# Row maxima of four attention heads: transposed at full array width and placed with one DMA

## The reference

```python
qkv = layernorm(x) @ w_attn + b_attn                # q, k, v: 32 heads of 16
scores = einsum('bqhd,bkhd->bhqk', q, k) / 16
scores = where(causal, scores + slope[h] * (k_pos - q_pos), -inf)
x = x + softmax(scores) @ v @ w_proj + b_proj
x = x + (silu(h @ w_gate.T) * (h @ w_up.T)) @ w_down.T     # h = layernorm(x)
```

## Time and profile before

| what | value |
|---|---|
| median of 3 executions | 840.43 us (840.23 to 841.11) |
| span of the profiled execution | 840.8 us |
| its own time | not given apart from the span, which lies among the three |
| TensorE busy | 789.2 us, 94% |
| VectorE, ScalarE, GpSimd busy | 646.3, 415.4, 296.3 us |
| mean granted TensorE clock | 0.994 of full |

### The profile page before, as it was taken

How to read it: one execution, slowest core, us unless ns; L and a number is a source line. 1 busy time by engine, 2 the same in 40 slices (tenths; PEclk the granted TensorE clock), 3 DMA queues, 4 the chain that set the end, 5 groups by cost and what they waited for, 6 DMA issues and landing times.

```text
span 840.8 us, 13423 instructions
## 1 busy us (share of the span) xinstructions
PE 789.2 (94%) x4554; PEld 543.8 (65%) x4554; DVE 646.3 (77%) x1609; ACT 415.4 (49%) x796; POOL 296.3 (35%) x435
## 2 busy tenths in 40 slices
PE   3899899999999999999998899999998999999998
PEld 2655455556555565555554477888876778888886
DVE  6497788878888888878887156849998787888764
ACT  4335666665666656565666524324336334334441
POOL 6223234342443424423433403324450034443342
PEclk9999999999999999999999999999999999999999
DMA  8873656556575575737563416041214422221052
GB/s 281 228 228 110 180 165 204 183 159 200 166 241 151 157 220 168 240 111 229 188 194 104 155 69 217 3 172 40 75 50 148 166 78 85 76 76 51 13 161 102
DMA packets 76332, 122.80 MB, mean 146 GB/s; under 512 B 14035, under 2 KB 39302, under 8 KB 76265
## 3 DMA queue, kind: packets, MB, share of 16 engines
q1 hardware_dynamic: 74217, 121.69, 45.9%
q10 hardware_dynamic: 2048, 0.27, 0.2%
HBM read 79.34 MB, written 42.32 MB: 145 GB/s over the span
## 4 chain that ended last, share of the span: by engine, by line
PE 62%; DVE 20%; DMA 6%; ACT 4%; issue 4%; POOL 2%; SPq 1%; ACTq 0%; DVEq 0%
PE bank L1282 19%; PE bank L1918 10%; PE bank L1201 7%; PE bank L1127 6%; PE bank L1184 6%; PE bank L1159 5%; PE bank L1112 5%; DVE bank L920 3%; PE bank L1116 3%; ACT pt L749 2%; DMA pv_dram<-weighed 2%; DVE stats L176 1%; POOL scratch L648 1%; DVE scratch L892 1%; PE bank L1094 1%
## 5 line engine op out<-in xcount | busy, mean ns | idle before, releaser
L749 ACT ACTIVATE pt<-bank 128x512 f32<-128x512 f32 (+1 forms) x384 | 193.8, 529 | 132.4 <-PE bank L1184 121.4
L920 DVE CUSTOM_DVE_ANT_0 bank<-bank,mask_qk 128x512 f32<-128x512 f32 (+3 forms) x416 | 195.9, 511 | 47.5 <-PE bank L1159 45.7
L1184 PE MATMUL bank<-q_st,k_st 116*128 116x512 bf16 (+3 forms) x512 | 133.6, 304 | 15.5 <-ACT pt L749 13.5
L1159 PE MATMUL bank<-k_st,q_st 97*128 97x512 bf16 (+3 forms) x512 | 133.1, 307 | 6.6 <-DMA q_st<-slopes_dram 4.3
L1513 POOL TENSOR_TENSOR wd_lo<-wd_raw,wd_hi 128x512 fp32r<-128x512 f32 x33 | 44.4, 1350 | 161.8 <-ACT wd_hi L1543 161.8
L654 POOL TENSOR_SCALAR_AFFINE_SELECT pt<-pt 128x256 f32<-128x256 f32 x128 | 55.6, 434 | 129.7 <-ACT pt L749 129.7
L1159 PEld LDWEIGHTS bank<-k_st,q_st 97*128 97x128 bf16 x512 | 42.2, 99 | 68.7 <-issue 38.4
L658 POOL TENSOR_SCALAR_AFFINE_SELECT pt<-pt 128x256 f32<-128x256 f32 x128 | 53.3, 416 | 77.0 <-ACT pt L749 76.7
L1201 PE MATMUL bank<-pt,v_nat 128*32 128x512 f32 (+3 forms) x1024 | 76.9, 441 | 3.0 <-POOL pt L654 2.3
L1184 PEld LDWEIGHTS bank<-q_st,k_st 116*128 116x128 bf16 x512 | 44.7, 98 | 47.3 <-ACT pt L749 23.5
L1918 PE MATMUL bank<-wd_hi,w_hi 128*128 128x512 f32 x176 | 70.0, 398 | 4.8 <-DVE wd_lo L1695 2.0
(11 more groups left out here) (185 smaller groups left out, 1714.8 us busy)
## 6 DMA issues: line engine op xcount, KB each, us to landing
stack_dram<-scratch SPq DMA_DIRECT2D x32, 384.0 KB, 3.1
q_st<-stack_dram SPq DMA_DIRECT2D x32, 384.0 KB
k_st<-stack_dram SPq DMA_DIRECT2D x32, 384.0 KB
wd_raw<-w_down SPq DMA_DIRECT2D x44, 256.0 KB, 3.5
xt<-w_gate_up SPq DMA_DIRECT2D x20, 512.0 KB, 3.7
stack_dram<-scratch SPq DMA_DIRECT2D x32, 256.0 KB, 3.6
pv_dram<-weighed SPq DMA_DIRECT2D x32, 256.0 KB, 4.4
weighed<-pv_dram SPq DMA_DIRECT2D x17, 256.0 KB
```

The lines of the kernel that those rows point to most:

```text
L749: act.activation(pt[:, h % PT_RING, COL0[k]:COL0[k] + WIDE[k]], bank[3 + (3 * h + k) % 2][:, 0:WIDE[k]], ACT.Exp, scale=1.0 / HD).then_inc ...
L920: last = dve.tensor_tensor_reduce(bank[k][:, at:at + n], bank[k][:, at:at + n], mask_qk[:, S - n:S], 1.0, NEG, ALU.add, ALU.max, mx[:, h % ...
L1159: last = pe.matmul(bank[k][:, at:at + n], q_st[0:K_MAX, s, h % 4, t * P:(t + 1) * P], k_st[0:K_MAX, s, h % 4, 0:n], start=True, stop=not b ...
L1184: last = pe.matmul(bank[3 + u % 2][:, at:at + n], k_st[0:K_EXP, s, h % 4, t * P:(t + 1) * P], q_st[0:K_EXP, s, h % 4, t * P:S], start=True ...
```

## The change

The 32 columns of `mparts` become the first columns of a 128-column tile `maxima`, whose other 96 columns are cleared once at the start by one more GpSimd memset. The transpose takes all 128 columns and writes 128 partitions of bank 6, the last 96 of them zeros. The copy takes the first 32 partitions, as before, to an `mt` with one buffer, and waits for the landing of the chunk before. One DMA takes 32 partitions of `mt` to rows 97 and 99, with one semaphore in place of two.

```diff
         mx = sb("mx", [P, 4, TT])
-        mparts = sb("mparts", [P, 2, 4 * TT], BF16)
-        mt = sb("mt", [2 * 4 * TT, 2, P], BF16)
+        maxima = sb("maxima", [P, P], BF16)
+        mparts = maxima[:, 0:2 * 4 * TT].rearrange("p (a n) -> p a n", a=2)
+        mt = sb("mt", [2 * 4 * TT, P], BF16)
...
-        m_placed = [sem(f"m_placed{i}") for i in range(2)]
+        m_placed = sem("m_placed")
...
-            pool.wait_ge(zeroed, 5)
+            pool.memset(maxima[:, :], 0.0).then_inc(zeroed, 1)
+            pool.wait_ge(zeroed, 6)
...
             def place_maxima(c):
-                n = 4 * TT
                 act.wait_ge(m_copied, c + 1)
-                for a in range(2):
-                    row = ROW_X + 1 + 2 * a
-                    act.dma_start(q_st[row:row + 1, c % SLOTS, :, :].rearrange("p h (t n) -> p (h t) n", n=P),
-                                  mt[a * n:(a + 1) * n, c % 2, :]).then_inc(m_placed[c % 2], 16)
+                act.dma_start(q_st[ROW_X + 1:K_SUM:2, c % SLOTS, :, :].rearrange("p h (t n) -> p (h t) n", n=P),
+                              mt[:, :]).then_inc(m_placed, 16)
...
             def copy_maxima(c):
                 dve.wait_ge(m_done, c + 1)
-                need(dve, m_placed[c % 2], c // 2 * 32)
-                dve.tensor_copy(mt[:, c % 2, :], bank[6][0:2 * 4 * TT, 0:P // 2].bitcast(BF16)).then_inc(m_copied, 1)
+                need(dve, m_placed, c * 16)
+                dve.tensor_copy(mt[:, :], bank[6][0:2 * 4 * TT, 0:P // 2].bitcast(BF16)).then_inc(m_copied, 1)
...
-                pe.transpose(bank[6][0:2 * 4 * TT, 0:P // 2].bitcast(BF16),
-                             mparts[:, :, :].rearrange("p a n -> p (a n)"), identb[:, :]).then_inc(m_done, 1)
+                pe.transpose(bank[6][:, 0:P // 2].bitcast(BF16), maxima[:, :], identb[:, :]).then_inc(m_done, 1)
...
                 if h % 4 == 0 and k == 0:
-                    pe.wait_ge(m_placed[c % 2], (c // 2 + 1) * 32)
+                    pe.wait_ge(m_placed, (c + 1) * 16)
```

## The result

The changed kernel took 837.8 us against 844.4 us of the kernel before, measured side by side in 20 executions each. The two medians differ by 6.5 us; the ratio of the executions is 0.993, with a 95% interval of 0.991 to 0.995, which is 5.9 us less. On other chips it gave 0.9924 (0.9894 to 0.9954) and 0.9938 (0.9910 to 0.9966). The forecast was 833 us, 0.9% less; the range, 829.5 to 838.5, holds the median by 0.7 us, though the kernel before itself came out 4 us higher than the 840.4 it was counted from. So the time itself tells little: rival 1's 837.0 lies nearer to it than the forecast. What tells the two apart is the difference and the profiles.

What follows compares the result with a forecast made beforehand. TensorE, busy 94% of the span and carrying 62% of the chain, was taken as the bound. Savings of 3.9 + 0.2 + 2.4 + 1.0 = 7.5 us from 840.4 gave 833 us, range 829.5 to 838.5.

Steps and rivals of the forecast that it cites:

- rival 1: The gap around TensorE's transpose comes from the bank or wait instructions, not the strip; 837.0 us, chance 0.12.
- Term 1: On TensorE, a full-width transpose avoids the 32-column strip's price: 0.195 us each at 20 chain places, 3.9 us, plus 0.2.
- Term 2: On ScalarE, one DMA issue in place of two saves 0.6 us at four places on the chain, 2.4 us.
- Term 3: Near 98 us, TensorE's wait for the placing's landing shrinks with one DMA: 1.0 us, between 0.55 and 1.35.
- Rival 2: The single placing DMA, shared by fewer DMA engines, lands late and costs time; about 844 us, chance 0.07.
- Rival 3: Half-clock stretches in the last chunks: one or both vanish, 831.3 or 829.6 (chance 0.12), or a third comes, 834.7 (0.06).

## Why the prediction was right

**Term 1, the transpose: right in its mechanism and in the size of one.** 0.26 us a transpose before and 0.06 after. At six of the 32 places, chunks 11, 12, 19, 20, 27 and 28, the distance shrank only to 0.29 to 0.32 us; what holds it there is open. The steady stretch gave 3.5 us, as the 18 transposes that the chain has in it times 0.195. The match is closer than the evidence: the three changed profiles have 310.8 to 312.7 us there without late round trips, and the full-width transpose with two DMAs 313.3. The division of the array was named as the cause from the strip products; 32, 64 and 128 columns, and one and two transposes, bear it out. The rule of the Trainium skill (TensorEngine Tiling (Array Packing), Key Properties) agrees, and these runs give its price here: about 0.10 us on the way in and 0.10 on the way out. Rival 1 is out: bank and waits were the same with the wide transpose, and the gap was gone.

**Term 2, the issue: the mechanism right, the size too high.** Forecast 0.6 us at each of four places, 2.4 in all. The kernel with the full-width transpose and two DMAs, beside the changed one, takes it alone. It is 0.5 us at each of the two places from 28 to 31 (34.9 against 33.9 us), because the single issue takes 0.62 us where the pair's took 0.51 and 0.60. It is 0.34 near 86 us (11.43 against 11.09 from transpose 3 to 4). Near 461 us it is 0.37 (6.70 against 6.33 from transpose 31 to the next value product). That makes 1.7 us.

**Term 3, the landing: the size right, its cause in part open.** 1.35 and 1.7 us of waiting before, 0.18, 0.19 and 0.35 in the three changed profiles: 1.0 to 1.5 for the 1.0 that was taken. But the wait is not the second DMA's alone. It is 0.40 us with two DMAs and the full-width transpose, 1.8 with two and the strip issued twice, 0.45 and 0.47 with one DMA and a strip, and 1.34 with one DMA and the full-width transpose issued twice. The last piece of this placing came 3.9 to 5.5 us after the first issue in the four profiles with two DMAs, 3.7 to 4.3 in six with one and 5.05 in a seventh. Over all chunks the medians are 3.2 to 3.5 us with two and 2.7 to 2.9 with one: the half microsecond that the forecast named is there, and this one placing scatters by more. The stretch from 1 to 5, with term 3 and one place of term 2 in it, gave 2.4 us for 2.0.

**Rival 2, the late landing, did not come,** but what it was built on did. The DMA queue of ScalarE moved 1088 pieces, as its page above has it, in place of the 2048 on the page of the kernel before:

```profile
q10 hardware_dynamic: 2048, 0.27, 0.2%
```

Sixteen pieces behind one another take some 0.3 us in most chunks, up to 1.3 in some. In the three changed profiles the last of them was moved 1.5 to 5.1 us after the issue, 2.8 in the median, where the rival needed a landing at 5.4 everywhere. One chunk of the kernel with its transpose issued twice has 5.7.

**Rival 3, the clock: partly seen, and no gain of the whole.** The kernel before has a half-clock stretch between transposes 28 and 31 in both profiles, the changed one in none of three. From 28 to 31 the kernel gained 2.4 us. The two parts by themselves, in kernels that have no half clock there either, make 1.2 us of it, as forecast: the strip costs 0.2 (34.1 against 33.9) and the second issue 1.0. The other 1.2 of the 2.4 is the clock's. But two of the three have it just behind transpose 31, and the part from there to the end is 1.1 us longer. In these two it was moved, not removed.

**The sum.** 3.5 for the steady stretch, 2.4 from 1 to 5, 2.4 from 28 to 31, less 1.1 behind it, is 7.2 us, against 7.5 forecast. That it comes so near is in part luck: the last two parts gave 1.2 more and 1.9 less than forecast, by where half-clock stretches fell. The three ratios give 5.2 to 6.4 us, and their intervals reach from 2.9 to 8.9. If the difference from 7.2 is more than scatter, the late round trips may be the place: mostly about 1.3 us each, and the changed profiles have one or two.

**What the forecast missed** is the scatter. It took 840.4 from three executions as the kernel's time; over 20 it was 844.4. Its upper bound, too, is 838.7 by its own terms (840.4 less 1.7), not 838.5. The start alone, up to the first transpose, varies from 46.4 to 50.9 us between profiles, a chunk with a late round trip by up to 3, the part behind transpose 31 by some 1.5 for each half-clock stretch.

## What to carry to other kernels

A small matmul that divides the array differently from its neighbours pays for the switch twice, on the way in and on the way out; this was measured here for a bf16 transpose of 128 rows and 32 or 64 columns. Look at the distance of starts around it, not at its own duration, and fill it up to its neighbours' width where the extra columns are free. Where a small transfer hangs behind a wait, count how often the engine that issues it, or its landing, is on the chain before taking a gain for it: here 4 and 1 of 32. Being on the chain is not the whole price: of four issues taken at 0.6 us, two gave 0.5 and two less than 0.4. And cut a profile into stretches at an instruction that recurs; parts of a change that the whole's scatter hides can be read there to a tenth of a microsecond where the stretch is short and holds no wait for a DMA and no half clock (11.16 and 10.66 us from transpose 29 to 30), and no better than 1 to 2 us over the long one from 5 to 28.

## What the runs showed of the hardware that was not expected

- A 64-column division costs as much as a 32-column one (0.44 us of spacing against 0.23 undivided), and a second transpose of the same division costs its columns only, 0.05 to 0.06 us.
- An 8 KB placing issued some 3 us later in a chunk was done sooner after its issue, 1.5 us in 21 of 32 chunks, where the earlier one took 2.8 in the median; in two chunks it took 4.0 and 4.4 us, behind the loads of tokens.
- One DMA on 2 engines, whose last piece moved 2.7 to 2.9 us after the issue (medians of seven profiles), was no later than two DMAs on 16 each, 3.2 to 3.5 us after the first issue (four profiles).
- The same wait for the same placing varied from 0.2 to 1.8 us between profiles, and not by the number of DMAs alone.
